# The product of Q with K·V in two row tiles of the PE array, each with a PSUM bank of its own

## The reference

```python
x = x + 0.5 * ffn(layernorm(x), w_gate_up, w_proj)
x = x + attn(layernorm(x), w_qkv, w_proj, b_proj)
x = x + 0.5 * ffn(layernorm(x), w_gate_up, w_proj)
```

```python
q, k = relu(to_heads(q)), relu(to_heads(k)); v = to_heads(v)
v_pad = pad(v, one more row of ones)                  # 33 rows per head
vk = einsum('bhen,bhdn->bhed', v_pad, k)              # 33 x 32 per head
out = einsum('bhed,bhdn->bhen', vk, q)                # 33 x tokens per head
out = out[:, :, :-1] / (out[:, :, -1:] + EPS)
return out.reshape(...).transpose(...) @ w_proj.T + b_proj
```

## Time and profile before

| | us |
|---|---|
| median of three runs | 892.62 |
| lowest and highest | 890.82, 892.72 |
| the profiled execution | 890.9 |
| its span, first to last instruction | 889.1 |
| TensorE busy in it | 874.6 |
| VectorE busy | 472.0 |
| ScalarE busy | 374.9 |
| matmuls of L1166 (both banks, 128 records) | 19.6 |

### The profile page before, as it was taken

How to read it: one execution, slowest core, us unless ns; L and a number is a source line. 1 busy time by engine, 2 the same in 40 slices (tenths; PEclk the granted TensorE clock), 3 DMA queues, 4 the chain that set the end, 5 groups by cost and what they waited for, 6 DMA issues and landing times.

```text
span 889.1 us, 12467 instructions
## 1 busy us (share of the span) xinstructions
PE 874.6 (98%) x4704; PEld 415.5 (47%) x4704; DVE 472.0 (53%) x950; ACT 374.9 (42%) x736; POOL 72.7 (8%) x107
## 2 busy tenths in 40 slices
PE   6899999999999999999999999999999999999998
PEld 5544444444444444455555555444444444444443
DVE  7899997824245445535464737453333444433232
ACT  6877667545334445212121213253334443433331
POOL 3210001200000000100000000000000010000000
PEclk7999999999999999999999999999999999999999
DMA  9999609996435687523322304054433343332235
GB/s 281 137 171 134 84 0 164 198 201 136 96 75 132 113 167 157 92 49 48 47 50 27 70 15 81 13 93 68 95 76 72 72 72 72 71 72 60 60 68 133
DMA packets 251387, 84.96 MB, mean 96 GB/s; under 512 B 237888, under 2 KB 240448, under 8 KB 251328
## 3 DMA queue, kind: packets, MB, share of 16 engines
q1 hardware_dynamic: 242704, 70.54, 42.8%
q0 software_dynamic: 3872, 4.72, 3.8%
q10 hardware_dynamic: 4752, 8.91, 3.0%
HBM read 25.43 MB, written 4.19 MB: 33 GB/s over the span
## 4 chain that ended last, share of the span: by engine, by line
PE 94%; DMA 2%; DVE 1%; SPq 1%; ACT 1%; issue 1%; ACTq 0%; DVEq 0%
PE proj_ps L1141 25%; PE gate_ps L1127 22%; PE up_ps L1127 22%; PE gate_ps L1237 7%; PE up_ps L1237 7%; PE proj_ps L1151 5%; PE proj_ps L1127 3%; DMA att_w<-aw_hl 1%; SPq L395 1%; PE gate_ps L1166 1%; PE up_ps L1166 1%; PE sum_ps L1113 1%; PE proj_ps L1252 1%; DMA xs<-in_L_attn_x_dram 1%; DMA xs<-xn 0%
## 5 line engine op out<-in xcount | busy, mean ns | idle before, releaser
L1141 PE MATMUL proj_ps<-down_w,slots 128*128 128x512 bf16 x960 | 211.3, 379 | 0.0
L1127 PE MATMUL gate_ps<-gu_w,xT 128*128 128x512 bf16 (+1 forms) x904 | 203.6, 368 | 1.3 <-DMA xT<-xn 1.3
L1127 PE MATMUL up_ps<-gu_w,xT 128*128 128x512 bf16 (+1 forms) x904 | 203.3, 368 | 0.0
L835 DVE SCALAR_TENSOR_TENSOR slots<-up_ps,silu 128x512 f32<-128x512 f32 x118 | 81.5, 691 | 176.1 <-PE up_ps L1127 154.2
L1141 PEld LDWEIGHTS proj_ps<-down_w,slots 128*128 128x128 f16 x960 | 94.0, 98 | 113.0 <-DVE xs L857 0.2
L587 ACT ACTIVATE silu<-gate_ps 128x512 f32<-128x512 f32 x118 | 69.6, 590 | 166.9 <-PE gate_ps L1127 166.6
L1127 PEld LDWEIGHTS gate_ps<-gu_w,xT 128*128 128x128 f16 x904 | 86.7, 98 | 101.4 <-DMA xT<-xn 1.7
L1127 PEld LDWEIGHTS up_ps<-gu_w,xT 128*128 128x128 f16 x904 | 86.1, 98 | 99.1
L597 ACT ACTIVATE o_buf<-slots 128x512 f32<-128x512 f32 x128 | 80.6, 630 | 99.9 <-DVE slots L835 99.3
L857 DVE SCALAR_TENSOR_TENSOR xs<-proj_ps,xs 128x512 f32<-128x512 f32 x32 | 22.1, 691 | 136.7 <-PE proj_ps L1141 136.7
L848 DVE SCALAR_TENSOR_TENSOR slots<-slots,inv 128x512 f16<-128x512 f32 x124 | 91.0, 744 | 2.8 <-ACT slots L608 2.8
(11 more groups left out here) (105 smaller groups left out, 733.0 us busy)
## 6 DMA issues: line engine op xcount, KB each, us to landing
out_dram<-xs SPq DMA_DIRECT2D x16, 256.0 KB, 2.3
slots<-in_L_ffn_w_gate_up_dram ACTq DMA_DIRECT2D x6, 512.0 KB, 7.5
aw_raw<-in_L_attn_w_qkv_dram ACTq DMA_DIRECT2D x12, 256.0 KB, 2.7
aw_raw<-in_L_attn_w_qkv_dram SPq DMA_DIRECT2D x12, 256.0 KB, 3.0
xs<-in_L_attn_x_dram SPq DMA_DIRECT2D x2, 1024.0 KB, 8.1
slots<-slots SPq DMA_TRANSPOSE x76, 4.4
xs<-in_L_attn_x_dram ACTq DMA_DIRECT2D x1, 1024.0 KB, 12.0
aw_raw<-in_L_ffn_w_gate_up_dram POOLq DMA_DIRECT2D x4, 256.0 KB, 8.3
```

What stands on the lines that cost most here:

```text
L835: nc.vector.scalar_tensor_tensor(out=h_rows(i, q), in0=bank(up_ps, j), scalar=gu_out(i), in1=silu_rows(j), op0=ALU.mult, op1=ALU.mult).the ...
L1127: mm = nc.tensor.matmul(bank(ps, j)[:, first:first + width], xT(m)[:, t, r, k, :], gu_w[:, k, c:c + width], start=(k + r == 0), stop=(k == ...
L1141: mm = nc.tensor.matmul(proj_ps[:, use % 2, :], h_turned(i)[:, r, j, :], down_w[:, j, :], start=(r + j == 0), stop=(r == 1 and j == HC - 1))
```

## The change

The array is used in two tiles of 64 rows. The upper tile takes the first two heads of every group (partitions 0 to 63) and writes gate_ps, the lower one the last two heads (partitions 64 to 127) and writes up_ps. `kv_rhs` shrinks from 132 to ROW_W = 66 columns per group: heads 0 and 2 of a group stand in its columns 0 to 32, heads 1 and 3 in columns 33 to 65, on their own partitions. There are 8 calls per `attention_output` where there were 4, each with 66 moving columns and 64 rows. The two banks' calls alternate, and both semaphores are raised in the last group. What the banks hold is now sorted by head pair within each group, so VectorE's product (L1038) writes into o_buf in four strips of 64 columns. The sizes in PSUM, 264 columns per bank, are as before, and so is ScalarE's copy. GpSimd zeroes 264 columns in place of 528.

```diff
--- before.py
+++ after.py
@@ -24,6 +24,7 @@
 HEADS = DC * HPG
 V_W = HEAD + 1
 KV_W = HPG * V_W
+ROW_W = 2 * V_W
 V_TILE = HEADS * V_W
 V_AT = TILES * D
 Q_AT = V_AT + TILES * V_TILE
@@ -186,7 +187,7 @@
         aw_raw = sb("aw_raw", [P, 2, D], F32)
         aw_hl = sb("aw_hl", [P, 2, D], F16)
         group_ones = sb("group_ones", [P, P], BF16)
-        kv_rhs = sb("kv_rhs", [P, DC, KV_W], F32)
+        kv_rhs = sb("kv_rhs", [P, DC, ROW_W], F32)
         den = sb("den", [P, DC * HPG], F32)
         stats = sb("stats", [P, TILES, 6], F32)
         mv = sb("mv", [P, 2 * TILES], F32)
@@ -1036,10 +1037,11 @@
                     dve.wait_ge(olo_done, TILES * b + max(t - 1, 0))
                 for s in range(2):
                     last = nc.vector.tensor_tensor(
-                        o_buf[:, t % 2, 256 * s:256 * s + 256].rearrange("p (h e) -> p h e", h=2 * HPG),
-                        halves[s][:, :, 0:HEAD],
-                        den[:, 8 * s:8 * s + 8].rearrange("p (h o) -> p h o", o=1)
-                        .broadcast_to([P, 2 * HPG, HEAD]), ALU.mult)
+                        o_buf[:, t % 2, :].rearrange("p (g s n) -> p s g n", g=DC, s=2)[:, s, :, :]
+                        .rearrange("p g (j e) -> p g j e", j=2),
+                        halves[s][:, :, 0:HEAD].rearrange("p (g j) e -> p g j e", g=DC),
+                        den[:, 8 * s:8 * s + 8].rearrange("p (g j o) -> p g j o", g=DC, o=1)
+                        .broadcast_to([P, DC, 2, HEAD]), ALU.mult)
                 last.then_inc(up_used, 1)
                 if t:
                     output_low(b, t - 1)
@@ -1059,7 +1061,7 @@
                         for e in range(HPG):
                             rows = slice(e * HEAD, e * HEAD + HEAD)
                             last = nc.vector.tensor_copy(
-                                kv_rhs[rows, :, e * V_W:e * V_W + V_W].rearrange("p (c g) m -> p c g m", c=2),
+                                kv_rhs[rows, :, e % 2 * V_W:e % 2 * V_W + V_W].rearrange("p (c g) m -> p c g m", c=2),
                                 proj_ps[rows, :, 0:2 * V_W].rearrange("p c (g m) -> p c g m", g=2))
                         last.then_inc(proj_used, 2)
                     dve.wait_ge(up_done, att_pair(b) + u + 1)
@@ -1159,13 +1161,17 @@
                     pe.wait_ge(gate_used, att_pair(b) + 6 + CREDIT)
                     pe.wait_ge(up_used, att_pair(b) + 6 + CREDIT)
                 j = att_pair(b) + 6 + t
-                for ps, done, used, g0 in ((gate_ps, gate_done, gate_used, 0), (up_ps, up_done, up_used, 2)):
+
+                halves = ((gate_ps, gate_done, gate_used, 0), (up_ps, up_done, up_used, 64))
+                for ps, done, used, row in halves:
                     pe.wait_ge(used, j + 1)
-                    for g in (g0, g0 + 1):
-                        c = (g - g0) * KV_W
-                        mm = nc.tensor.matmul(ps[:, j % 2, c:c + KV_W], q_chunk(g)[:, t * P:(t + 1) * P],
-                                              kv_rhs[:, g, :], start=True, stop=True)
-                    mm.then_inc(done, 1)
+                for g in range(DC):
+                    for ps, done, used, row in halves:
+                        mm = nc.tensor.matmul(ps[:, j % 2, g * ROW_W:(g + 1) * ROW_W],
+                                              q_chunk(g)[row:row + 64, t * P:(t + 1) * P],
+                                              kv_rhs[row:row + 64, g, :], start=True, stop=True)
+                        if g == DC - 1:
+                            mm.then_inc(done, 1)
 
             def turn_first(p):
                 pe.wait_ge(first_here[p], 16)
```

## The result

| | before | after |
|---|---|---|
| median of six runs, us | 892.31 | 895.13 |
| lowest and highest | 890.82, 892.72 | 894.51, 895.99 |
| span of the profiled execution | 889.1 | 893.0 |

The ratio is 1.0033, with a 95% interval of 1.0021 to 1.0046: slower by 2.8 us, and by 1.9 to 4.1 with the interval. The direction was forecast, and the time lies within the range that was given (893 to 902 us around 896.9). The size of 4.3 us is half again the measured 2.8, and lies a little above the interval.

A forecast was written before the change was run, and what follows sets the result against it. TensorE, busy 98% of the span, was taken as the bound. Steps +0.6 us and entering and leaving tiled mode +3.7 made +4.3, on the median of 892.62 giving 896.9 us, within 893 to 902 (889.0 to 904.5 with most rivals).

The forecast's parts named there:

- What bounds the kernel: Attention stage: TensorE, busy 98% of the span, is the bound; time gained or lost in its matmuls reaches the end.
- Do row tiles work side by side: Row-tiled calls of attention_output: both tiles run in parallel and load next weights under the current matmul, as in keys_values.
- in series: Rival for attention_output: the row tiles share the way in, 256 loads of 112.5 ns, 910.7 us; chance 0.12.
- no background load: Rival for attention_output: a row tile loads only after its matmul, 164 ns a step, 902.2 us; chance 0.08.
- The step: Matmul to matmul in one tile of attention_output: load 109 plus 8 ns surcharge, 117 against 112.5; +0.6 us over 128 steps.
- Entering and leaving: Ends of tiled runs in attention_output: 0.09 ahead, 0.11 behind, 0.065 exposed, 0.265 us per run; 14 runs, +3.7 us.
- no change: Rival: switching between 128 and 64 rows costs next to nothing, the step stays 109 to 112 ns, 893.1 us; chance 0.12.
- The sign for one output: Expected in the trace: one output between plain matmuls takes about 1.16 us, 0.90 before.
- The late gate bank: gate_ps finishes later, ScalarE's copy starts about 0.6 us later; 0.56 us cover leaves VectorE below 0.1 us; cost zero.
- VectorE's products: VectorE's two products per output write four strips of 64; even 10% more is 0.08 us per step; cost zero.
- The matmul's duration: Expected in the trace: matmul records of the row-tiled line near 221 ns, from 276 less 132 columns.
- The rule of the Trainium skill: Load time goes by columns, supporting the forecast step; the packed-tile span without loads alone would give near 61 ns.

The follow-up runs named there:

- e1_quarters: Changed kernel with each call split into two column tiles of 64 stationary columns, four 64x64 tiles: 889.18 us against 891.99 for the kernel before.
- e4_wide_rows: Changed kernel with 132 moving columns per row-tiled call in place of 66, results wrong, only time counts: 897.06 us against 891.99 for the kernel before.
- e8_eighths: Changed kernel with each call split into four column tiles of 32 stationary columns, eight 64x32 tiles: 891.73 us against 891.32 for the kernel before.
- e7_quarters_pairs: Changed kernel with four 64x64 tiles, and two projections then two outputs in blocks 1 to 3: 887.11 us against 891.32 for the kernel before.

## Why the prediction held, point by point

**What bounds the kernel.** Right. All that the stage added came through to the end: 3.43 us in the stage, nothing returned behind it.

**Do row tiles work side by side.** Right. The argument from L1252, four column tiles, carried over to row tiles: 0.01 us between their starts. Neither "in series" (steps of 225) nor "no background load" (164) is in the trace.

**The step.** The mechanism was right and its size was off. The load sets it, as e1_quarters and e4_wide_rows show. But the surcharge over the 109 ns of the load, taken as a constant 8 ns from the 35 ns of L1252, is 3 ns here: 112 in place of 117 (and 58 over 55 in e1_quarters). The term was +0.6 us and measured -0.1, and it is the largest part of the error against the trace. The fault most likely lay in reading the 8 ns as a property of loads. In e8_eighths 128 instructions took 5 ns each, which is about what the 256 of L1252 took; with 32 instructions in 0.90 us the change is far from that pace. The prediction had named this as a possible part of the 35 ns. Of its bounds for the step, the one without surcharge was the nearer.

**Entering and leaving.** 0.25 us per run against 0.265, 14 x 0.25 = 3.5 us against 3.7. The 0.09 ahead and the 0.11 behind, read at 32-column tiles, hold for row tiles: 440.70 to 440.79 ahead, and the next plain group again takes 2.70 in the chain. The "no change" rival rested on a cheaper switch and is out.

**The sign for one output.** The prediction gave 1.16 us for one output, and 1.15 came. But its own terms, 8 x 0.117 + 0.265, make 1.20; the parts that it listed beside the 1.16 leave out the exposed ends. The close hit is luck: the figure that follows from the forecast is 0.05 us too high, which is the surcharge again.

**The sum.** -0.1 + 3.5 = 3.4 us by the trace, against 4.3. The medians give 2.8, and their interval (1.9 to 4.1) holds the trace's 3.43. The difference between 2.8 and 3.43 is not explained by anything in the traces and is within the noise.

**The late gate bank.** The cover was counted too generously: 0.17 us of wait on VectorE, not below 0.1, because the copy began 0.58 us later against L865 (the cover was 0.56) and 0.14 us pass between its end and VectorE's start (449.79 to 449.93). That it costs nothing was right in this kernel. But the reason given, that TensorE needs the bank again only 7 us later, does not hold at the end of a block, where the next `qkv` takes it after one more output. In the faster e7_quarters_pairs it does cost.

**VectorE's products.** 0.42 us each as before, though they write four strips.

**The matmul's duration.** 221 ns was expected and 272 measured. The matmul's record begins before the record of its own load has ended:

```profile
448.37 0.19 PEld L1170 LDWEIGHTS gate_ps<-kv_rhs,slots 64*128 64x128 f32 x1
...
448.42 0.27 PE L1170 MATMUL gate_ps<-kv_rhs,slots 64*128 64x66 f32 x1
```

So its length tells of the load as well. In e1_quarters, with half the load, it is 218, near the expected 221.

**The rule of the Trainium skill.** The step is the load's and the load takes 188 ns with 64 rows against 190 with 128. That agrees with the section LDWEIGHTS of "TensorE: Matmul & The Clock Gate", by which columns and not contraction rows count; the span of packed tiles without a term for loads (Part 3 of that page) does not describe this case, where a step would be near 61 ns by it (an estimate) and is 112.

## What to carry to other kernels

In these kernels a matmul step is the longer of load and stream, and with float32 operands of 128 stationary and 132 moving columns the two are about equal (109 and 110 ns): a tiling that halves only one of them gains nothing and pays 0.25 us for each run of tiled calls. Halve both, keep the tiled calls together, and alternate the tiles call by call, but stop where more and smaller calls no longer shorten an output (0.73 us with four tiles, 0.90 with eight). Before splitting, work out the step from both the load's and the matmul's duration in the trace.

## What the runs showed of the hardware that was not expected

- A change between plain and tiled calls costs the same for 64x128, 128x64 and 128x32 tiles: some 0.09 us ahead and 0.10 to 0.11 behind, beside a first load or a last matmul that nothing hides.
- Issuing all eight matmuls of one tile ahead of the other's costs 0.50 us per output (1.64 against 1.15), as if the tiles shared one queue in program order.
- 128 load and matmul instructions in eight tiles took 0.65 us, 5 ns each, where load and stream alone would allow 0.46.
- The duration in a tiled matmul's record seems to include waiting for its weights: 272 ns with a load of 128 columns and 218 with 64, at the same 66 moving columns, and 272 again with 132 moving columns and the load of 128.
